# A language-model tower on one core: GpSimd and ScalarE in another order round the low parts, sequence 1 turned by TensorE

## The reference

```python
h = take(weight, x) * take(keep_mask, x)
n = layernorm(h)
u, res = split(n @ in_proj_w.T, [512])            # 512 + 256
u = causal_conv1d(u, conv_w, 4 taps, depthwise) + conv_b
delta = softplus(u @ dt_proj_w.T + dt_proj_b)
y = scan(state = 0.9 * state + 0.1 * (u * sigmoid(delta)))   # along the tokens
h = h + y @ out_proj_w.T + res
n = layernorm(h); xd = dequantise(fp6_blocks_of_32(n)); wd = the same of ffn_weight
h = h + xd @ wd.T + ffn_bias
```

## Time and profile before

| what | value |
|---|---|
| median of 3 runs | 1024.26 us (1023.52 to 1025.87) |
| the profiled execution, its own time | 1026.02 us |
| its span (first to last instruction) | 1024.2 us |
| mean granted clock of TensorE | 0.988 |
| busy: TensorE, VectorE, GpSimd, ScalarE | 955.7, 829.8, 750.3, 647.2 us (93, 81, 73, 63%) |
| DMA moved | 100.81 MB |

### The profile page before, as it was taken

How to read it: one execution, slowest core, us unless ns; L and a number is a source line. 1 busy time by engine, 2 the same in 40 slices (tenths; PEclk the granted TensorE clock), 3 DMA queues, 4 the chain that set the end, 5 groups by cost and what they waited for, 6 DMA issues and landing times.

```text
span 1024.2 us, 14964 instructions
## 1 busy us (share of the span) xinstructions
PE 955.7 (93%) x4892; PEld 781.8 (76%) x4892; DVE 829.8 (81%) x1218; ACT 647.2 (63%) x1342; POOL 750.3 (73%) x749
## 2 busy tenths in 40 slices
PE   2689999999999999999999999999999999999996
PEld 1476887777877778787777788777878787878885
DVE  4767988888888888898888888888889878889866
ACT  5755666666667766666676666766666666665541
POOL 6647777777787777878777788777787787776652
PEclk9889999999999999999999999999999999999998
DMA  5213432244433234443223443323444322343101
GB/s 170 69 35 103 123 91 81 88 115 124 124 103 95 77 93 123 123 123 102 77 88 103 123 123 108 94 76 91 123 123 123 102 68 88 112 124 103 62 23 42
DMA packets 73790, 100.81 MB, mean 98 GB/s; under 512 B 12577, under 2 KB 61089, under 8 KB 73761
## 3 DMA queue, kind: packets, MB, share of 16 engines
q1 hardware_dynamic: 67616, 83.59, 25.7%
q0 software_dynamic: 6144, 16.85, 7.2%
HBM read 51.65 MB, written 48.76 MB: 98 GB/s over the span
## 4 chain that ended last, share of the span: by engine, by line
POOL 41%; issue 21%; DVE 20%; PE 9%; ACT 7%; DMA 1%; POOLq 0%; DVEq 0%; ACTq 0%
POOL g_lo L381 16%; POOL rows L366 11%; DVE u L757 10%; POOL xT_lo L430 5%; ACT n L558 4%; DVE h L767 3%; DVE stats L773 3%; POOL rstd L415 3%; POOL h L425 3%; ACT u L515 2%; PE psZ L1074 1%; PE psZ L1068 1%; PE psZ L1067 1%; POOL nmr L419 1%; POOL u_lo L388 1%
## 5 line engine op out<-in xcount | busy, mean ns | idle before, releaser
L757 DVE SCALAR_TENSOR_TENSOR u<-psU,cw,u 128x511 f32<-128x511 f32 x378 | 260.0, 741 | 82.6 <-ACT u L515 80.2
L388 POOL TENSOR_TENSOR u_lo<-u,u_hi 128x512 fp32r<-128x512 f32 x128 | 164.5, 1296 | 83.1 <-ACT u_hi L522 79.0
L1074 PE MATMUL psZ<-u_lo,dt_hi 128*128 128x512 f32 x512 | 208.9, 408 | 12.5 <-POOL u_lo L388 12.5
L381 POOL TENSOR_TENSOR g_lo<-g,g_hi 128x512 fp32r<-128x512 f32 x128 | 199.8, 1580 | 20.6 <-ACT g_hi L533 19.9
L1067 PE MATMUL psZ<-u_hi,dt_hi 128*128 128x512 f32 x512 | 201.4, 393 | 5.7 <-ACT u_hi L522 4.6
L1068 PE MATMUL psZ<-u_hi,dt_lo 128*128 128x512 f32 x512 | 202.2, 395 | 0.0
L522 ACT ACTIVATE u_hi<-u 128x512 fp32r<-128x512 f32 x128 | 81.0, 633 | 138.4 <-DVE u L757 137.7
L366 POOL DMA_INDIRECT rows<-table,ids x128 | 127.1, 993 | 44.9 <-issue 44.1
L1074 PEld LDWEIGHTS psZ<-u_lo,dt_hi 128*128 128x128 f32 x512 | 96.5, 188 | 58.9 <-POOL u_lo L388 40.7
L515 ACT ACTIVATE u<-psU,cb,cw 128x512 f32<-128x512 f32 x126 | 94.3, 772 | 39.7 <-PE psU L1010 39.6
L533 ACT ACTIVATE g_hi<-g 128x512 fp32r<-128x512 f32 x128 | 76.6, 621 | 62.3 <-DVE g L837 62.3
(11 more groups left out here) (120 smaller groups left out, 2215.5 us busy)
## 6 DMA issues: line engine op xcount, KB each, us to landing
turned_n<-nb_blocks SPq DMA_DIRECT2D x31, 512.0 KB
nT<-turned_n SPq DMA_DIRECT2D x124, 128.0 KB
out<-h SPq DMA_DIRECT2D x31, 512.0 KB, 4.6
turned<-xb SPq DMA_DIRECT2D x30, 512.0 KB, 2.6
xT<-turned SPq DMA_DIRECT2D x120, 128.0 KB, 2.9
rows<-table,ids POOLq DMA_INDIRECT x128
dt_stage<-dt_wT SPq DMA_DIRECT2D x1, 1024.0 KB, 5.8
g<-in_wT SPq DMA_DIRECT2D x1, 768.0 KB
```

The lines of the kernel that those rows point to most:

```text
L381: pool.tensor_tensor(g_lo[:, m, :], g[:, m, :], f32(g_hi[:, m, :]), ALU.subtract).then_inc(g_lo_ready[m], 1)
L388: pool.tensor_tensor(u_lo[:, m, :], u[:, m, :], f32(u_hi[:, m, :]), ALU.subtract).then_inc(u_lo_ready[m], 1)
L757: dve.scalar_tensor_tensor(u[:, m, back:T], u_psum_tile(st, m)[:, 0:T - back], cw[:, m, TAPS - 1 - back:TAPS - back], u[:, m, back:T], ALU ...
L1074: ins = pe.matmul(psZ[:, m % 2, :], dt_hi[:, k, o], u_lo[:, k, :], start=False, stop=(k == M - 1))
```

## The change

- GpSimd: `split_g(3)` goes ahead of `add_bias`, `mean1(2)` behind `split_u(1)`, `split_xT` ahead of `split_u(2)`, `variance1(2)` and `inverse_root1(2)` behind `split_u(3)`. The low part of the dt weight is made in four pieces.
- ScalarE: `split_xT` ahead of taps 2 and 3, `square1_rows(2)` behind them.
- Sequence 1 is masked and normalised in step 0 and turned by TensorE (between `dt_proj(2)` and `dt_proj(3)`) instead of through DRAM; its statistics come from VectorE. Sequence 2 is masked and squared at the end of step 0, normalised early in step 1, and is the first to go through DRAM. Semaphore counts for `nT_lo` and `n_turned` are one lower.
- Start: each gathered chunk of sequence 0 has its own semaphore, and the weight loads wait for the first chunk alone. The output weight's split and the ffn weight's comparison move into step 0. Step 0 convolves channel by channel.
- Step 1: `linear_lo` ahead of `convolve` of channels 2 and 3.
- End: `gate(2)` between `block_scale` and `inverse_scale` in step 31; `split_xT` on VectorE ahead of `add_h` in step 32, the last half's `split_xT` ahead of `add_linear`; the last sequence's `add_bias` waits for `xd_ready` instead of `n2_ready`.

```diff
@@ semaphores and SP
+        first_gathered = [sem(f"first_gathered{c}") for c in range(C)]
+        def gathers(ring, turn):
+            return GATHERS * (turn - 1 if ring == 0 else turn)
-                self.turn_ahead = (1, 2) if self.first else (2,) if self.early else ()
+                self.turn_ahead = () if self.first else (1, 2) if self.second else (2,) if self.early else ()
-            sp.wait_ge(gathered[0], GATHERS)
+            sp.wait_ge(first_gathered[0], 16)
@@ GpSimd, step
+                if st.back:
+                    split_g(M - 1, s - 1)
                 if st.tail:
                     add_bias()
-                if st.back:
-                    split_g(M - 1, s - 1)
-                if st.first:
-                    variance1(1)
-                    inverse_root1(1)
-                if st.early:
-                    mean1(2)
                 split_u(0)
                 split_u(1)
-                if st.early:
+                if st.early and not st.first:
+                    mean1(2)
+                if st.tail:
+                    split_xT()
+                split_u(2)
+                split_u(3)
+                if st.first:
+                    inverse_root1(1)
+                elif st.early:
                     variance1(2)
                     inverse_root1(2)
-                split_u(2)
-                split_u(3)
-                if st.tail:
-                    split_xT()
...
                 split_g(2, s)
+                if st.first:
+                    mean1(2)
+                    variance1(2)
+                    inverse_root1(2)
...
-            pool.tensor_tensor(dt_lo[:], dt_stage[:], f32(dt_hi[:]), ALU.subtract).then_inc(dt_lo_ready, 1)
+            for k in range(M):
+                pool.tensor_tensor(dt_lo[:, k, :], dt_stage[:, k, :], f32(dt_hi[:, k, :]),
+                                   ALU.subtract).then_inc(dt_lo_ready, 1)
@@ GpSimd, add_bias
+                        if part is None:
+                            pool.wait_ge(n2_ready, s - 1)
+                        else:
+                            pool.wait_ge(xd_ready, s)
@@ ScalarE
                     mask_rows(1)
                     normalise1(1)
-                    mask_rows(2)
                     split_nT()
...
+                if st.first:
+                    first_tap(0)
+                    mask_rows(1)
+                    first_tap(1)
+                    first_tap(2)
+                    first_tap(3)
+                    for m in range(M):
+                        split_u(m)
+                    tanh(0)
+                    normalise1(1)
+                    tanh(1)
+                    split_g(0)
+                    tanh(2)
+                    split_nT()
+                    split_g(1)
+                    out_proj_hi()
+                    mask_rows(2)
+                    split_g(2)
+                    tanh(3)
+                    square1_rows(2)
+                    return
...
                 if st.second:
                     linear_hi()
+                    normalise1(1)
                 split_u(0)
                 split_u(1)
                 if st.early:
                     mask_rows(2)
-                    square1_rows(2)
-                if not st.first:
-                    first_tap(2)
-                    first_tap(3)
                 if st.tail:
                     split_xT()
+                first_tap(2)
+                first_tap(3)
+                if st.early:
+                    square1_rows(2)
                 split_u(2)
                 split_u(3)
@@ VectorE
                         scan(1)
+                        split_xT(None)
                         add_h(0)
...
-                        split_xT(None)
                         block_max(0)
...
+                if st.first:
+                    convolve(0, 0, 0, 1, 1, 1)
+                    convolve(2, 2, 2, 3, 3, 3)
+                    statistics1()
+                    variance1()
+                    gate(0)
+                    compare_weight()
+                    gate(1)
+                    choose_weight()
+                    split_nT()
+                    gate(2)
+                    out_proj_lo()
+                    return
                 convolve(0, 1, 0, 1, 0, 1)
-                if st.first:
+                if st.second:
                     turn_n1(1)
                 if st.back:
                     scan(0)
                     scan(1)
-                convolve(2, 2, 3, 2, 3, 3)
                 if st.second:
                     linear_lo()
+                convolve(2, 2, 3, 2, 3, 3)
@@ TensorE
                 dt_proj(2)
+                if st.first:
+                    pe.wait_ge(first_nT_lo, 1)
+                    transpose_n1()
                 dt_proj(3)
```

More of the change, by code:

```diff
@@ L335, in step @@
                     ring, turn = st.ring(0)
-                    sp.wait_ge(gathered[ring], GATHERS * turn)
+                    if st.first:
+                        for c in range(C):
+                            sp.wait_ge(first_gathered[c], 16)
+                    else:
+                        sp.wait_ge(gathered[ring], gathers(ring, turn))
                     sp.dma_start(ids[:, ring, :], x[s + 4]).then_inc(ids_loaded[ring], 16)
@@ L440, in step @@
                     return
-                def gather_ahead():
-                    ring, turn = st.ring(3)
-                    gather(ring, ring, range(C))
                 if st is lead_in:
@@ L476, in step @@
                 if st.gather:
-                    gather_ahead()
+                    gather(ring, [gathered[ring]] * C)
                 split_g(0, s)
@@ L537, in mask_rows @@
                     ring, turn = st.ring(ahead)
-                    act.wait_ge(gathered[ring], GATHERS * turn)
+                    if st is not lead_in:
+                        act.wait_ge(gathered[ring], gathers(ring, turn))
                     for c in range(C):
+                        if st is lead_in:
+                            act.wait_ge(first_gathered[c], 16)
                         ins = act.activation(h[:, ring, c, :], h[:, ring, c, :], ACT.Copy,
@@ L565, in normalise1 @@
                     act.wait_ge(nmr1_ready, s + ahead + 1)
+                    by_pe = s + ahead < 2 if isinstance(s, int) else False
+                    if st.first and ahead == 1:
+                        n1_free(1)
                     for c in range(C):
                         to, h_c = n1[:, c, :], h[:, ring, c, :]
-                        if st is not lead_in:
+                        if not by_pe:
                             to, h_c = n1_blocks[:, :, :, c, :], h_c.rearrange("p (k q j) -> p k q j", k=KD, q=Q)
@@ L910, in turn_n1 @@
                     dve.wait_ge(n1_ready, s + ahead + 1)
-                    if not (st.first and ahead == 1):
-                        dve.wait_ge(n_written, 16 * (s + ahead - 1))
+                    if not (st.second and ahead == 1):
+                        dve.wait_ge(n_written, 16 * (s + ahead - 2))
                     dve.transpose(nb_blocks[:], flat(n1[:])).then_inc(n_turned, 1)
@@ L916, in split_nT @@
                     dve.wait_ge(nT_hi_ready, s + 2)
-                    if st is not lead_in:
+                    if st is not lead_in and not st.first:
                         dve.tensor_tensor(by_token(nT_lo[:, nb]), nT_by_token, f32(by_token(nT_hi[:, nb])),
@@ L961, in step @@
                     block_max(None)
-                    quantise()
+                    block_scale(None)
+                    if not st.front:
+                        gate(2)
+                    inverse_scale(None)
+                    round_to_grid(None)
                     dve.wait_ge(q_ready, s)
-                gate(2)
+                if st.front:
+                    gate(2)
                 if st.back and not st.front:
```

95 lines of the change are left out of this document (43 added, 52 removed).

## The result

| | before | forecast | after |
|---|---|---|---|
| median of 3 runs, us | 1024.26 | 1027.5 | **1054.42** (1051.59 to 1054.51) |
| span of the profiled execution, us | 1024.2 | 1027.4 | 1049.7 |
| up to `turn_n1` of step 2 | 109.97 | 101.2 | 99.98 |
| one steady step (27 of them) | 30.23 | 30.8 | 31.53 |
| from `turn_n1` of step 29 to the end | 98.0 | 94.6 | 98.5 |

The ratio after to before is 1.0283, with a 95% interval of 1.025 to 1.0315. The range of the forecast, 1010 to 1042, doesn't hold it. Of the difference of 26.9 us, 22.3 lies in the span: -1.2 in the start, 27 x (31.53 - 30.80) = +19.7 in the steady steps, +3.9 in the end.

The account below looks back on a forecast made before the run. A closed round without idle time was the bound; its successor, 30.26 + 0.4 + 0.15, gives 30.8 us a step. Steps +15.4, start -8.8, end -3.4 sum to +3.2 on 1024.26: 1027.5 us, range 1010 to 1042.

Parts of the forecast that it names:

- The round of 30.26: Steady step: new closed round from `turn_n1(2)` (start called T) through taps, `convolve`, `u_lo(3)`, root and `normalise1`: 30.26 us.
- The collision: Steady step: GpSimd's `g_lo(0)` and `g_lo(1)` meet VectorE's `block_scale` and `round_to_grid`; net +0.4 us a step.
- the 0.38 of `dequantise`: Steady step: `dequantise` then runs clear of GpSimd, 1.22 us for 1.60, a gain of 0.38.
- the bound of +1.5: Upper bound of the net +0.4 a step: the rounding held through both `g_lo`.
- `round_to_grid` stretched to 1.8: Sign in the new trace: VectorE's `round_to_grid` takes 1.8 us instead of 1.2.
- rival 1: Steady step: locks fall otherwise and `xT` is in time; 30.2 to 30.5 a step, 1011 to 1020 us; chance 0.30.
- xT_hi, +0.15: Steady step: ScalarE wants `xT_hi` about when its DMA lands; +0.15 us a step, bounds 0 and +0.5.
- The start, -8.8: Up to `turn_n1` of step 2: 101.2 us instead of 109.97, -8.8; bounds -12 and -5.
- The end, -3.4: Last steps: TensorE gets work 1.5 us earlier, VectorE's changes count some 1.9; -3.4 us, bounds 0 and -6.
- TensorE as the bound: Rival 2, steady step: all stalls gone, 29.5 us a step, 993 us; chance 0.10, shared with a 1002 us case.
- The rival on the other side: Another name for rival 1: 30.2 to 30.5 us a step, 1011 to 1020 us; chance 0.30.
- Rival 3: Steady step: `nT_lo` holds up the second gather, `g_lo` comes late; 31.4 us a step, 1044 us; chance 0.16.

Follow-up runs that it names:

- e1: Kernel after, with GpSimd's `variance1(2)` and `inverse_root1(2)` back ahead of `split_u(2)` from step 1 on: 971.59 us, ratio 0.9466.
- e5: Kernel after, with ScalarE's `split_xT` behind taps 2 and 3 again, in every step: 1033.23 us, ratio 1.0073.
- e12: Kernel after, with ScalarE's `split_xT` behind taps 2 and 3 in the last two steps alone: 1051.35 us, ratio 1.0238.
- e3: Kernel after, with GpSimd's and ScalarE's steady orders of the kernel before; new start and end stay: 1014.69 us, ratio 0.9887.
- e10: Kernel after, with one more wait: GpSimd starts `g_lo(1)` only when `dequantise` is done: 1018.84 us, ratio 0.9933.
- e9: Kernel after, with GpSimd's fourth gather moved between `g_lo(0)` and `g_lo(1)`: 1052.65 us, ratio 1.0256.
- e11: Kernel before, with GpSimd's `variance1` and `inverse_root1` moved behind `u_lo(3)` from the second step on: 1217.08 us, ratio 1.1861.

## Why the prediction was wrong, point by point

- **The round of 30.26: right.** From the end of the first `convolve` (522.90 + 4.01) to the next `turn_n1` it is 14.46 us after; the forecast was 14.31 and 0.15 for `xT_hi`, 14.46 (the last 0.15 by luck, see below). That the reordering "takes one round apart and closes another of the same length" is what e1 shows: the other one opened as well, the step is 28.71.
- **The collision: right in place, wrong in size, and this is the step that failed.** "Net **+0.4** a step" rested on step 30 of before, where `block_scale` took 0.43 and got its turn between two `g_lo`. In the steady steps it doesn't: it takes 1.80, `block_scale` to `dequantise` is 4.16 us (519.81 - 515.65) instead of the 3.37 forecast, +0.79 a step, with the 0.38 of `dequantise` gained as said. The net is +1.2, near the bound of +1.5 that the text gave. 27 x 0.73 = 19.7 of the 22.3 us in the span are this term. The text also had `round_to_grid` stretched to 1.8; it was `block_scale`, right before it, so the sign that it gave for rival 1 (`round_to_grid` not stretched) came true in the steady steps while that rival didn't.
- **Why step 30 was a bad witness.** There nothing is gathered, and `g_lo(0)` begins after a pause of 2.71 us; `block_scale` got its turn at the end of the first `g_lo`. In the steady steps of the kernel after the same `g_lo` stands right behind a gather, and there it gets it only at the end of the row, in 26 of 27 steps; in the other one (862.08) it runs during the gather, and `round_to_grid` behind it takes 3.70. The trace of the kernel before has no `g_lo` that follows a gather, isn't held up itself and meets a VectorE instruction, so the size couldn't be read from it; the text had it in its bounds. Between +0.4 and the bound of +1.5, 27 times, lie 30 us.
- **xT_hi, +0.15: no wait was there.** `xT_hi` waited 0.28 and 0.12 us for its DMA in two early steps and not at all in the other steady ones. The 0.15 lies in the links instead, 0.10 of it between the end of `normalise1` (539.15 + 2.09) and `turn_n1` (541.37), where the forecast had 0.03. The sum was right by luck.
- **The start, -8.8: -10.0 measured**, within its bounds, and by the path forecast: the taps of step 1 stand behind the squares (49.97 instead of 51.1), `turn_n1` of step 1 comes at 68.63 instead of 70.8, and the step after it takes 31.35 instead of 30.4. With the old steady order it is -11.1; the same start varies by 2.5 us from trace to trace.
- **The end, -3.4: +0.5 measured.** With GpSimd's new order the end takes 94.7 and 95.1 us once `xT_hi` stands behind the taps (e5, e12); what was missed is that taps 2 and 3 there hang on a landing whose write took 4.8 us. Before, the same write took 2.6 and nothing stood behind it. Why it takes longer is open. The store of `out` just ahead of it doesn't explain it: it is issued 4.0 us ahead in the kernel after; in e3 it is 5.1 ahead and the write takes 4.3 us, in e10 3.5 ahead and it takes 2.6. Nor is it shown that the gains come from VectorE's new end, as forecast: e3 has that too, and its end takes 98.0.
- **Rivals.** TensorE as the bound was right to fall here, and is right for e1. The rival on the other side, locks that fall well (30.2 to 30.5), is what e10 makes with a wait. Rival 3, the held gathers, came in a mild form: the third, issued under `nT_lo`, takes 1.22 instead of 0.95 in each step read; the first `g_lo` still starts when forecast, at T + 5.05.

## What to carry to other kernels

When GpSimd and VectorE work on SBUF at once, find each row of GpSimd instructions with no gap between them and each VectorE instruction issued in it. Price the latter twice, at the end of the one instruction and at the end of the row; in these traces it was the end of the row where the row follows a gather. Where it lies on the path, make GpSimd wait for it: a wait made two of these kernels 3% and 11% faster. A small instruction on the path (here the root, 1.5 us) belongs ahead of long ones that it doesn't need, and what it is moved behind is added to every round that runs through it. A row of the trace is a witness only for steps that run the same instructions round it: here step 30, without gathers, stood for 27 steps with them.

## What the runs showed of the hardware that I had not expected

- GpSimd can keep a VectorE instruction waiting over a whole row of its own. It was held 1.6 us through the rest of one `g_lo` and another, 1.6 through half a gather and a `g_lo` (e9), and 6.2 through three `g_lo` and a bias (e11, 7.4 us in all). The Trainium skill (SBUF — State Buffer, Who interferes with whom) says of a VectorE instruction in one of its two-port modes that, of it and one of GpSimd, whoever issues first gets the shared ports for the whole instruction, while the other blocks fully. The trace of the kernel after agrees that `block_scale` blocks fully, but not on the length: it outlasts two instructions. Whether `block_scale` runs in such a mode no run here shows.
- In other rows VectorE gets its turn between two of them: `dequantise` in 27 steps of the kernel before (1.60 us instead of 1.22), `block_scale` in step 30 (0.43). The rows where it had to wait for the end follow a gather; why is open.
- A gather, too, keeps a VectorE instruction waiting: `round_to_grid`, issued 0.53 us into one of 0.96, was held (e9). Issued 0.28 into one it ran at once (e3, 1.23 us). A gather is itself held by VectorE: 1.90 instead of 0.95 in e11, where it is issued 0.14 behind `round_to_grid`.
- A `block_scale` of 0.18 us cost 1.80, more than the 1.23 of the rounding on 1024 columns: what an instruction costs beside the other engine doesn't go by its size.
